# One state-space stage, redistributed: four B-products made transposed, GpSimd weighing seven states, the residual joined one stage later

## What is computed

```python
def step(h, inp):
    dt_t, u_t, B_t, C_t = inp
    dA = jnp.exp(dt_t[:, :, None] * A)
    h = dA * h + (dt_t * u_t)[:, :, None] * B_t[:, None, :]
    y = jnp.einsum('bdn,bn->bd', h, C_t)
    return (h, y)
...
y = y + u * D_param
y = y * jax.nn.silu(z)
return y @ W_out.T + residual
...
h = _layernorm(x) * (1 + ca) + sa
x = x + ga * _L1_attn(h)
h = _layernorm(x) * (1 + cb) + sb
x = x + gb * _L1_ffn(h)
```

## Time and profile before

| | us |
|---|---|
| median of three runs (4103.15 to 4108.57) | 4107.88 |
| span of the profiled execution | 4108.2 |
| profile: setup, layer 0 | 0 to 1990 |
| profile: `state_space` | 1990 to 3918 |
| profile: `experts` | 3918 to 4108 |

### The profile page before, as it was taken

The page is one execution under the profiler, slowest core; times in us unless marked ns, Lnnn a source line. Parts: engine busy times, 40 slices in busy tenths (PEclk is TensorE's granted clock), DMA queues, the critical chain, the costliest instruction groups (busy, mean ns, idle before and its releaser), DMA issues. The chain is left out here.

```text
span 4108.2 us, 61159 instructions
## 1 busy us (share of the span) xinstructions
PE 3305.6 (80%) x21708; PEld 1529.2 (37%) x21708; DVE 3549.2 (86%) x5829; ACT 2321.0 (56%) x4302; POOL 2624.4 (64%) x2459
## 2 busy tenths in 40 slices
PE   5979999999993999999566777777777777776467
PEld 3633333333332555555322232222232232222166
DVE  5768888888854999999359999999999999999967
ACT  5626666666672344444356666666666666666422
POOL 1102323232232888888369999999999999998723
PEclk8969999999996999999888888888888888887689
DMA  4894565655513111110112222212222222222132
GB/s 146 281 188 64 78 84 79 88 80 81 82 33 89 35 44 45 44 48 30 34 44 61 63 65 64 69 47 60 69 65 64 65 69 61 68 57 53 42 95 85
DMA packets 274957, 299.58 MB, mean 73 GB/s; under 512 B 35583, under 2 KB 205686, under 8 KB 274646
## 3 DMA queue, kind: packets, MB, share of 16 engines
q1 hardware_dynamic: 274654, 295.68, 31.4%
HBM read 210.22 MB, written 84.51 MB: 72 GB/s over the span
## 5 line engine op out<-in xcount | busy, mean ns | idle before, releaser
L1727 POOL TENSOR_TENSOR d_dBu<-d_dtu,d_Bn 128x1024 f32<-128x1024 f32 x512 | 1217.5, 2413 | 0.1
L1562 ACT ACTIVATE d_dA<-d_dt,d_decay 128x512 f32<-128x512 f32 x1024 | 690.9, 687 | 404.4 <-DVE d_h L1810 402.1
L752 ACT ACTIVATE b_P<-b_pT 128x512 f32<-128x512 f32 (+1 forms) x1120 | 571.8, 575 | 298.1 <-PE b_pT L658 295.3
L1810 DVE TENSOR_TENSOR_SCAN d_h<-d_dA,d_last_h,d_dBu 128x512 f32<-128x512 f32 x512 | 617.1, 1265 | 14.5 <-ACT d_dA L1562 12.8
L1810 DVE TENSOR_TENSOR_SCAN d_h<-d_dA,d_dBu 128x512 f32<-128x512 f32 x512 | 586.3, 1204 | 40.3 <-ACT d_dA L1562 39.0
L785 DVE CUSTOM_DVE_ANT_0 b_pS<-b_pS,mask_qk 128x512 f32<-128x512 f32 (+1 forms) x768 | 501.7, 690 | 83.6 <-PE b_pS L668 74.3
L630 POOL TENSOR_SCALAR_AFFINE_SELECT b_P<-b_P 128x128 f32<-128x128 f32 (+2 forms) x608 | 192.8, 321 | 515.0 <-ACT b_P L752 503.2
L668 PE MATMUL b_pS<-KS,QS 99*128 99x512 bf16 (+3 forms) x1536 | 475.0, 339 | 28.5 <-PEq L85 21.6
L658 PE MATMUL b_pT<-QS,KS 118*128 118x512 bf16 (+3 forms) x1536 | 449.1, 329 | 3.1 <-ACT b_P L752 2.1
L1817 DVE TENSOR_TENSOR d_h<-d_h,d_C 128x2048 f32<-128x2048 f32 x192 | 434.4, 2262 | 0.7 <-PE d_C L1446 0.7
L1446 PE MATMUL d_C<-d_bc,d_pick 96*128 96x512 bf16 x256 | 114.6, 448 | 396.1 <-DVE d_h L1817 396.1
(11 more groups left out here) (313 smaller groups left out, 5983.2 us busy)
## 6 DMA issues: line engine op xcount, KB each, us to landing
d_Bn<-scratch_bs SPq DMA_DIRECT2D x128, 512.0 KB, 4.9
scratch_parts<-a_part SPq DMA_DIRECT2D x48, 512.0 KB, 4.1
QS<-scratch_parts SPq DMA_DIRECT2D x192, 128.0 KB, 7.4
KS<-scratch_parts SPq DMA_DIRECT2D x192, 128.0 KB, 7.9
scratch_v<-a_v SPq DMA_DIRECT2D x16, 1024.0 KB, 7.7
V<-scratch_v SPq DMA_DIRECT2D x32, 512.0 KB, 11.7
a_x<-in_L_attn_x_dram SPq DMA_DIRECT2D x16, 512.0 KB, 7.7
scratch_o<-b_O SPq DMA_DIRECT2D x16, 512.0 KB, 10.0
```

The source lines that it names most:

```text
L752: act.activation(t[:, heads[0]:heads[-1] + 1, c * CH:c * CH + w], pT[:, place % RING, 0:len(heads) * w].rearrange("p (h w) -> p h w", w=w) ...
L1562: act.activation(dA[:, m % 2, :], dt[:, c.k % 2, m, :], ACT.Exp, scale=decay[:, m, n:n + 1]).then_inc(dA_d, 1)
L1727: pool.tensor_tensor(product(c, n)[:, 2 * j:2 * j + 2, :], dtu[:, c.k % 2, 2 * j:2 * j + 2, :], Bn[:, n // BG % 2, n % BG, :].unsqueeze(1) ...
L1810: dve.tensor_tensor_scan(h[:, n % HS, m, :], dA[:, m % 2, :], product(c, n)[:, m, :], start, ALU.mult, ALU.add).then_inc(scanned, 1)
```

## The change

- **B-products of four states** (PE_B = 5, 8, 11, 14). POOL makes only the other twelve. For these four, dt·u and B are first turned to [token, channel] (`turn_step`, `turn_b` on PE; `put_step`, `put_b` on ACT). ACT then makes the product of state `of` as four activations with a scale per token (`stage_product`, one in each half of iterations of - 2 and of - 1), PE turns it back tile by tile into the two PSUM slots of dA (`turn_product`, four transposes per m), and the decays of these states go to a new SBUF buffer dAs.
- **C.** POOL_C = (0, 2, 3, 6, 9, 10, 12): POOL weighs seven states, DVE nine. POOL's C rows now come by DMA from memory (SP's `spread_c`, three buffers), ACT's `evacuate_c` and PE's matmuls for those states are gone. `take_x` rows for C are stored with those of B.
- **Input.** The multiplication in `modulate` goes from DVE (n = 4) to POOL (n = 6). DVE's statistics go from n = 6 to 7, ACT's `normalise(f, 1, ...)` one half to one iteration later.
- **Residual.** `finish` is gone: the gated output (h1e) is stored as a3, and `experts` loads x2 and a3 and adds them on POOL (`join`).

```diff
-POOL_C = (0, 3, 6, 11)
+PE_B = (5, 8, 11, 14)
+POOL_C = (0, 2, 3, 6, 9, 10, 12)
...
@@ PE @@
             def spread(c, e, n):
+                if n in PE_B and c is not None:
+                    turn_product(c, n, (0, 1))
                 if n > 0 and c is not None:
                     spread_c(c, n - 1)
...
+                    turn_product(c, n, (2, 3))
+                if n == 1 and c is not None:
+                    turn_b(c)
                 if n == 2 and c is not None:
+                    turn_step(c)
+                if n == 3 and c is not None:
+                    wait(pe, dtuT_put, c.times(2, 2))
                     sum_blocks(lambda i, m: diag[i * QB:(i + 1) * QB, m, :], u, True, False).then_inc(y0_mm, 1)
+            def turn_step(c):
+                wait(pe, dtu_d, c.times(1, 1))
+                wait_before(pe, yz_d, c.times(1, 0), passed)
+                for t in range(CT):
+                    for m in range(MD):
+                        last = pe.transpose(y[:, t, m * P:(m + 1) * P], dtu[:, c.k % 2, m, t * P:(t + 1) * P], K["ident"][:, :])
+                    if t % 2:
+                        last.then_inc(dtuT_mm, 1)
+            def turn_product(c, n, halves):
+                i = PE_B.index(n)
+                wait(pe, staged, c.times(CT * NPE, CT * i + CT))
+                for m in halves:
+                    wait(pe, scanned, c.times(NS * MD, MD * n + m - 1))
+                    for t in range(CT):
+                        last = pe.transpose(dA[:, m % 2, t * P:(t + 1) * P], product(c, n)[:, t, m * P:(m + 1) * P], K["ident"][:, :])
+                    last.then_inc(turned_b, 1)
@@ ACT @@
+            def stage_product(c, n, half):
+                for i, of in enumerate(PE_B):
+                    if of - 2 <= n < of:
+                        t = 2 * (n + 2 - of) + half
...
+                        act.activation(product(c, of)[:, t, :], dtuT[:, t, :], ACT.Identity, scale=BT[:, t, of:of + 1]).then_inc(staged, 1)
+            def put_step(c, j):
+                wait(act, dtuT_mm, c.times(2, j + 1))
+                act.activation(dtuT[:, 2 * j:2 * j + 2, :], y[:, 2 * j:2 * j + 2, :], ACT.Copy).then_inc(dtuT_put, 1)
...
             def first_two(c, e, n):
...
-                    if n - 1 in POOL_C:
-                        evacuate_c(c, n - 1)
+                    stage_product(c, n, 0)
+                    if n == 1:
+                        put_b(c)
+                    if n == 2:
+                        put_step(c, 0)
             def last_two(c, e, n):
                     for m in (2, 3):
                         step_decay(c, n, m)
+                    stage_product(c, n, 1)
+                    if n == 2:
+                        put_step(c, 1)
@@ POOL @@
-                ({15: finish}, {14: step_input}, {6: shift, 8: scale_bias_first}))
+                ({}, {14: step_input}, {6: modulate, 9: scale_bias_first}))
@@ DVE @@
-                 {4: modulate, 6: stats, 13: clear}))
+                 {7: stats, 13: clear}))
@@ POOL, experts @@
+            def join(n):
+                wait(pool, x_in[n % XS], n // XS * 32 + 32)
+                pool.tensor_tensor(x[:, n % XS, :, :], x[:, n % XS, :, :], a[:, n % AS, :, :], ALU.add).then_inc(x3_d, 1)
+            join(0)
             def step(f, g_, d, c):
...
                 if c is not None:
                     wait(pool, og_d, c + 1)
                     pool.tensor_tensor(x[:, c % XS, :, :], x[:, c % XS, :, :], og[:, c % 2, :, :], ALU.add).then_inc(out_d, 1)
+                if f is not None and f + 1 < total:
+                    join(f + 1)
@@ DVE, experts @@
                 if f is not None:
-                    wait(dve, x_in[f % XS], f // XS * 16 + 16)
+                    wait(dve, x3_d, f + 1)
                     for t in range(2):
                         dve.bn_stats(st[:, f % 2, t, :], x[:, f % XS, t, :])
```

More of the change, by code:

```diff
@@ L1271 @@
 NQB = P // QB
-POOL_C = (0, 3, 6, 11)
+PE_B = (5, 8, 11, 14)
+POOL_B = tuple(n for n in range(NS) if n not in PE_B)
+POOL_C = (0, 2, 3, 6, 9, 10, 12)
 DVE_C = tuple(n for n in range(NS) if n not in POOL_C)
@@ L1275 @@
 SUM_ORDER = [n for sums in SUMS for n in sums]
-HS, BG, BS = 4, 2, 3
+HS, BG, BS, CR = 4, 2, 3, 3
+NPE, NPB, NPC, NDC = len(PE_B), len(POOL_B), len(POOL_C), len(DVE_C)
+MADE = [2 * sum(i < n for i in POOL_B) for n in range(NS + 1)]
 def state_space(nc, A, S, K):
@@ L1403, in step @@
[L1403 to L1412, removed]
+                for n in range(NS):
+                    if n == 0 and f is not None:
+                        load(f)
+                    if c is not None:
+                        if n % BG == 0 and 0 < n < NS - BG:
+                            spread_next(c, n // BG + 1)
+                        for j in range(CR, NPC):
+                            if POOL_C[j - CR] + 3 == n:
+                                spread_c(c, j)
+                    if n == 8 and f is not None:
+                        wait(sp, h1_d, f.times(1, 1))
+                        sp.dma_start(tiles(S["r"][tokens(f), :]), h1[:, :, :]).then_inc(h1_st, 16)
+                    if n == 10 and q is not None:
+                        wait(sp, act_read, q.times(NF, WX + 1))
+                        sp.dma_start(S["bs"][:, tokens(q)], xb[DR:DR + 2 * NS, :]).then_inc(b_st, 16)
@@ L1724, in unit @@
                     wait(pool, b_in[g % 2], c.times(8 * NS // BG, 16 * (g // 2) + 16))
-                for j in range(2):
-                    wait(pool, scanned, c.times(NS * MD, MD * (n - BS) + 2 * j + 2))
+                for j in range(2 if n in POOL_B else 0):
+                    wait(pool, scanned, before(c, n) if (n - BS) % NS in PE_B else c.times(NS * MD, MD * (n - BS) + 2 * j + 2))
                     pool.tensor_tensor(product(c, n)[:, 2 * j:2 * j + 2, :], dtu[:, c.k % 2, 2 * j:2 * j + 2, :],
@@ L1756, in scale_bias_first, with modulate @@
                     scale_bias_x(slice(CT, B * QT), 1)
-            def shift(f):
+            def modulate(f):
+                wait(pool, m_in[f.k // 2 % 2], f.over(4, 16, 16))
+                wait(pool, xn1, f.times(1, 1))
+                pool.tensor_tensor(x[:, :, :], x[:, :, :], row(f, CA), ALU.mult).then_inc(h_mul, 1)
                 wait(pool, h_mul, f.times(1, 1))
-                wait(pool, m_in[f.k // 2 % 2], f.over(4, 16, 16))
                 wait(pool, xn2, f.times(1, 0))
@@ L1836, in stats @@
                 last.then_inc(stat, 1)
-            def modulate(f):
-                wait(dve, m_in[f.k // 2 % 2], f.over(4, 16, 16))
-                wait(dve, xn1, f.times(1, 1))
-                dve.tensor_tensor(x[:, :, :], x[:, :, :], row(f, CA), ALU.mult).then_inc(h_mul, 1)
             def clear(f):
@@ L1946, in step @@
                     load(1)
-                if f is not None and f + 2 < total:
-                    load(f + 2)
+                    load(2)
+                if f is not None and f + 3 < total:
+                    load(f + 3)
                 if c is not None:
```

142 lines of the change are left out of this document (85 added, 57 removed).

## The result

The median went from 4107.88 to **4376.22 us** (four runs of each; 4374.14 to 4384.55 now): 1.066 times the time before, 95% interval 1.064 to 1.067. The forecast was 4226 and its range ended at 4285. The sign is right, the size is not: 268 us lost where 118 were forecast. The profiled execution spans 4371.8 us.

A forecast was written before the change was run, and what follows sets the result against it. DVE was taken to bound state_space, busy 108.7 of 111.6 us a chunk; less work but more waits made 114.6. 4108.2 + 35 (state_space) + 83 (experts) = 4226 us, range 4065 to 4285.

The forecast's parts named there:

- DVE's work: In state_space, three weighings and modulate leave DVE: 108.7 - 8.1 = 100.6 us of work a chunk.
- the walk: Following the four engines' lists through one even chunk of state_space: DVE waits of 14.0 us a chunk against 2.9.
- state 4: In state_space, ACT's staging, convolved and normalise delay decays (4,0) and (4,2): DVE waits 1.3 and 0.7 us.
- 14: State 14 in state_space: first transposes stand behind PE's project(GT + 3), which waits for ACT's gate(2): 2.4 us of wait.
- 6: State 6 in state_space: PE, held in turn_product(5), does the last convolution late, so decay (6,0) is late: 1.4 us.
- State 7's cover: In state_space, the statistics (1.84 us) move behind the scans of 7 and no longer cover silu; wait at 7: 3.5 us.
- `experts`: In experts, bn_stats waits 4.95 us for join, a step grows to 14.2, and PE's lower clock adds 2.7: +83 us.
- rival 3: The join is harmless: experts stays at 190 us and the sum is 4143; chance 0.01.
- Rivals 1: Rival 1: the stalls in state_space stay hidden, period 103.5 us, time 4029 to 4062; chance 0.14.
- 2: Rival 2: half the stalls in state_space stay hidden, period 107 to 111 us, 4110 to 4190 in all; chance 0.16.
- Rival 4: PE at half clock in state_space: states 6, 11 and 14 add some 3 us each, +126, 4350; chance 0.06.
- the rule cited there: The Trainium skill's statement that PE transposes do not count as activity for the clock.

The follow-up runs named there:

- run 2: The changed kernel with POOL weighing each state in two instructions of 1024 columns instead of one of 2048: 4293.35 us.
- run 11: The changed kernel with join before the og wait, POOL's weighings and step_input in halves, modulate at 5, statistics at 6, splits at 10 and 13: 4155.84 us.
- Run 12: The kernel of run 11 with convolved(q, 0) on ACT moved from the end of iteration 2 to behind decays (3, 0) and (3, 1): 4133.2 us.
- run 6: The kernel before with only DVE's statistics moved from iteration 6 to 7: 4154.29 us against 4106.36.
- run 5: The changed kernel with modulate on POOL at iteration 5 and the statistics on DVE back at iteration 6: 4361.4 us.
- Run 1: The changed kernel with POOL's join(f + 1) in experts done before the wait for og instead of after x += og: 4298.3 us.
- run 10: The kernel before with only POOL's weighing done as two instructions of 1024 columns: ratio 1.001 to the kernel before.
- run 3: The changed kernel with project(q, GT + 3) on PE moved from the end of iteration 13 to behind turn_product(14): 4399.45 us.

## Why the prediction was wrong, step by step

- **DVE's work** is the step that failed first: "100.6 us a chunk" took away 8.1 and left every other instruction at its old duration; 2.5 came off. POOL's three added weighings were costed on POOL alone. The two splits grew by 4.9 us together, of the 5.6 by which the work missed. The other 0.7 lies in no instruction's length: the lengths add up to 3.5 us less a chunk, near 8.1 - 4.9 = 3.2, but DVE's instructions overlap less than before. Shown by runs 2 and 11, and by where the splits end in all traces. The row that gave it away was quoted in the prediction itself: `modulate` at 6.89 "beside POOL", and L2069 at 0.95 for 0.2. I used the first to credit the change and the second as a term in `experts`, and asked of neither which other DVE instructions would stand beside POOL afterwards.
- **The waits** are the second: the walk gave 14.0 and the profile has 18.1. Means over ten chunks beside the walk's terms: state 4 1.79 (2.0), 7 3.46 (3.5), 11 2.54 (2.8): right; 2 1.14 (1.4). Mis-sized: 14, 4.10 against 2.4, since the projection ran at the lower level (3.51 for 1.96), and 6, 1.92 against 1.4. Missing: state 3, 1.30, and state 9, 0.84. At 3 `convolved(q, 0)` overwrites u and waits for y0, which the change puts behind `put_step` and, in PE's list, behind `convolve(q, 0)`. I moved y0 and did not follow who waits for it. Run 12 shows it: without that order the wait at 3 is gone. State 9 was not followed up. At 6 the wait is 1.1 to 1.2 us in six of the ten chunks and 3.4 in three, where the last convolution ran slowly. PE and DVE in such a chunk, and PE in the next:

```profile
3000.40 5.76 PE L1585 MATMUL d_f<-d_xi,d_cdiag 128*128 128x512 f32 x8
3007.61 4.81 DVE L1895 TENSOR_TENSOR_SCAN d_h<-d_dA,d_last_h,d_dBu 128x512 f32<-128x512 f32 x4 [3.44 <-ACT d_dA L1625]
```

```profile
3126.61 3.60 PE L1585 MATMUL d_f<-d_xi,d_cdiag 128*128 128x512 f32 x8
```

- **State 7's cover** (1.84 of statistics) is confirmed by run 6 in the kernel before, 1.83 at the scans of 7, and by run 5 in the changed one.
- **`experts`**: +83, measured +84. A step of 14.2 + 2.7 = 16.9 with the clock, measured 17.05 (4249.72 to 4266.77; the twelve steps average 16.8); `bn_stats` 4.95 later, measured 4.8. Run 1 gave back 78, so rival 3 was rightly dismissed for this order, and would have been right for the other.
- **Rivals 1 and 2** fell: the waits were not hidden. **Rival 4** came true in part: the projection ahead of 14 in every whole chunk, the convolution ahead of 6 in three of ten. Together they cost some 2.2 us a chunk and not 9, and the granted clock over the ten chunks is 0.83, 0.86 before. What the transposes did to that clock no run separates, so the rule cited there stays open.
- **The range** reached to 4285 by a spread on the waits only. The work was taken as certain, and it was the term that moved most.

## What to carry to other kernels

When work goes to GpSimd, list the VectorE instructions with two SBUF operands that will stand beside it, and cost each at what is left of the GpSimd instruction when it arrives, at worst the full length. Dividing the long GpSimd instructions bounds that cost (83 us in run 2) and gives nothing where the neighbour arrives late anyway (run 10). When an operation is moved, follow not only what it waits for but who waits for it, and the list of each consumer: runs 3 and 12 are the same mistake with either sign. A long instruction or a weighing in the right place is cover, so removing work pays only where no wait is behind it.

## What of the hardware was not expected

A DVE instruction of 0.7 us took 4.25 beside a POOL instruction of 4.53, and 2.08 beside the same work in two. The disturbance goes by what is left of the neighbour, to within 0.04 us: the split ends 0.54 to 0.58 us after it. It is mutual (5.13 us for 4.68 on POOL). DVE's weighings, with C in PSUM, don't feel it: all 144 of the changed kernel lie between 2.258 and 2.287 us.

```profile
L1902 DVE TENSOR_TENSOR d_h<-d_h,d_C x144: 2258/2262/2287, 2113.3 to 4071.2; 128x2048 f32<-128x2048 f32 x144
```
